# A kernel of resampled pointwise MLP and selective scan: D's row blocks in four places, S in two, `wtot` at slot 60, and a new slot plan

## What is computed

```python
def _L0(x):                                   # layer 0
    xu = upsample_rfft(x)                     # band-limited, twice per axis
    h = xu @ W1.T + b1                        # 96 -> 384
    h = coef[:, 0] + coef[:, 1] * h + coef[:, 2] * (h * h)
    h = h @ W2.T + b2                         # 384 -> 96
    return lpf_rfft(h)[..., ::2, ::2]         # back to 64 x 64
def _mamba(u):                                # layer 1, 4096 tokens in order
    xs, z = split(u @ W_in.T)                 # 192 + 192
    xc = silu(causal_conv3(xs) + conv_b)
    dt, Bm, Cm = split(xc @ W_x.T)            # 6, 16, 16
    delta = softplus(dt @ W_dt.T + b_dt)
    h = exp(delta * A) * h + delta * Bm * xc  # a scan over tokens, 192 x 16 states
    return ((h * Cm).sum(-1) + xc * D) * silu(z) @ W_out.T
x = x + _L0(_gn(x))                           # _gn: group norm, groups of 3 channels
x = x + _mamba(_gn(x))
```

## Time and profile before

| | |
|---|---|
| median of 3 runs | 6460.34 us (6443.52 to 6460.46) |
| the profiled execution | 6467.2 us; its span 6465.4 us |
| first `b` of the loop starts | 343.86 us |
| instructions | 99088 |
| mean granted TensorE clock | 0.951 |
| DVE scans | 3072, 1262 ns each |

### The profile page before, as it was taken

One profiled execution on the slowest core, in us unless ns is written; L12 is line 12 of the kernel. 1 busy time (PEld: TensorE's weight loads), 2 busy tenths in 40 slices (PEclk: granted clock), 3 DMA queues, 4 the chain that ended last, 5 costly groups with the idle time before them and its releaser, 6 DMA issues. The chain is left out here.

```text
span 6465.4 us, 99088 instructions
## 1 busy us (share of the span) xinstructions
PE 6103.6 (94%) x32316; PEld 3160.6 (49%) x32316; DVE 5686.3 (88%) x4459; ACT 5099.6 (79%) x8658; POOL 5211.7 (81%) x5092
## 2 busy tenths in 40 slices
PE   7999999999999999999999999999999999998776
PEld 5645545455454544545455544545545454454222
DVE  0089998999999999999989999898999989899998
ACT  4587888878788887878888788887878888786664
POOL 0078888888888888888888888888888888888988
PEclk8999999999999999999999999999999999998675
DMA  3276666666666667676666766666676666766553
GB/s 91 81 169 164 159 163 150 161 162 166 163 151 161 152 168 162 162 171 146 167 152 160 171 151 168 149 162 157 164 166 154 163 151 165 157 144 148 128 129 74
DMA packets 805826, 983.26 MB, mean 152 GB/s; under 512 B 391258, under 2 KB 417542, under 8 KB 805318
## 3 DMA queue, kind: packets, MB, share of 16 engines
q1 hardware_dynamic: 805318, 976.92, 64.3%
HBM read 717.71 MB, written 259.00 MB: 151 GB/s over the span
## 5 line engine op out<-in xcount | busy, mean ns | idle before, releaser
L1145 POOL TENSOR_TENSOR hc<-hs,cs 128x512 f32<-128x512 f32 x3072 | 3838.8, 1273 | 799.2 <-DVE hs L1104 467.2
L1104 DVE TENSOR_TENSOR_SCAN hs<-av,state,b 128x512 f32<-128x512 f32 x2688 | 3254.7, 1262 | 83.0 <-DVE b L1098 1.8
L974 ACT ACTIVATE av<-rep_d,nega 128x512 f32<-128x512 f32 x3072 | 2113.1, 713 | 34.4 <-DVE hs L1104 29.9
L1098 DVE TENSOR_TENSOR b<-rep_u,pb 128x1536 f32<-128x1536 f32 x1024 | 1802.5, 1760 | 249.7 <-PE pb L813 169.8
L822 PE MATMUL py<-hc,rsel 128*32 128x512 f32 x6144 | 1142.5, 634 | 64.6 <-POOL hc L1145 63.0
L738 PE MATMUL cb<-xu,w1a 96*128 96x392 f32 x2400 | 996.1, 517 | 23.1 <-ACT g L924 9.2
L743 PEld LDWEIGHTS cb<-w2c,g 128*98 128x98 f32 x9600 | 893.3, 169 | 163.2 <-issue 94.6
L743 PE MATMUL cb<-w2c,g 128*98 128x96 f32 x9600 | 917.2, 253 | 14.5 <-ACT g L924 11.7
L777 PE MATMUL cb<-xn,wtap 96*96 96x512 f32 x1536 | 737.4, 617 | 0.0
L924 ACT ACTIVATE g<-cb,b1a 128x392 f32<-128x392 f32 x1200 | 674.1, 579 | 66.8 <-PE cb L738 59.9
L738 PEld LDWEIGHTS cb<-xu,w1a 96*128 96x128 f32 x2400 | 417.3, 192 | 422.4 <-issue 231.4
(11 more groups left out here) (104 smaller groups left out, 6721.8 us busy)
## 6 DMA issues: line engine op xcount, KB each, us to landing
rep_d<-delta_scratch SPq DMA_DIRECT2D x512, 384.0 KB, 6.9
rep_u<-deltax_scratch SPq DMA_DIRECT2D x512, 384.0 KB, 6.6
cs<-c_scratch SPq DMA_DIRECT2D x512, 256.0 KB, 5.9
delta_scratch<-dlt SPq DMA_DIRECT2D x128, 384.0 KB, 3.1
deltax_scratch<-dlt SPq DMA_DIRECT2D x128, 384.0 KB, 7.7
t_scratch<-t1s SPq DMA_DIRECT2D x128, 300.0 KB
t1r<-t_scratch SPq DMA_DIRECT2D x160, 240.0 KB, 6.2
rr<-v_scratch SPq DMA_DIRECT2D x256, 150.0 KB
```

The lines of the kernel that those rows point to most:

```text
L974: act.activation(av[:, n % NAV, :], rep_d[:, k % 2, j, :], ACT.Exp, scale=nega[:, q, j:j + 1])\
L1098: dve.tensor_tensor(b3[:, :, :], rep_u[:, k % 2, 3 * hf:3 * hf + 3, :], pb[:, None, :].broadcast_to([128, 3, T]), ALU.mult).then_inc(dve_b ...
L1104: dve.tensor_tensor_scan(hs[:, n % NHS, :], av[:, n % NAV, :], b3[:, n % 3, :], start, ALU.mult, ALU.add)\
L1145: pool.tensor_tensor(hc[:, n % NHC, :], hs[:, n % NHS, :], cs[:, k % 2, g % NQ, :], ALU.mult)\
```

## The change

It sets other slots: X at 8 and 10, Z1 at 11, Z0 at 12, DBC at 14, S to slot 87, W from 105, D from 100 to 139, ACT's `xn` and `d` at 10 and 11, POOL's `bc` and `y` at 18, 22 and 17, 8; no slots are kept free. DVE's lag is 3. A new unringed step DW at slot 60 has POOL make `wtot`; DG waits for `act_w` alone, and the first D_lo waits for `pool_w`. D's row blocks take four places, two of `rr` and two of `xb`, loaded four ahead. `xs` alternates with a half of `x1s`, and `t1s` with `rr`, each with a semaphore of its own. At the start SP loads `ident`, x block 0, `up_w` and x block 1 first, PE begins the S steps of sample 0 when these are there, and PE's, ACT's and part of DVE's setup stands behind those steps.

```diff
@@ -35,13 +35,13 @@
...
-    "act": dict(xn=8, y=(18, 6), d=13, mid=23, batch=16),
+    "act": dict(xn=10, y=(18, 6), d=11, mid=23, batch=16),
...
-    "pool": dict(u=23, bc=(17, 20), y=(18, 9)),
-    "sp": dict(rd=(1, 2, 3, 4), ru=(7, 9, 11, 13), cs=(15, 16, 17, 18), dl=20, du=3, x1=19, out=23),
+    "pool": dict(u=23, bc=(18, 22), y=(17, 8)),
+    "sp": dict(rd=(1, 2, 3, 4), ru=(7, 9, 11, 13), cs=(15, 16, 17, 18), dl=21, du=4, x1=21, out=23),
...
-LAG = {"pe": 0, "act": 4, "dve": 2, "pool": 1, "sp": 1}
-UNRINGED = ("SLD", "WLD", "DLD", "WARM")
+LAG = {"pe": 0, "act": 4, "dve": 3, "pool": 1, "sp": 1, "bn": 3}
+UNRINGED = ("SLD", "WLD", "DLD", "DW", "WARM")
@@ -71,15 +71,16 @@
...
-S_LAST, W_FIRST, W_LAST, D_FIRST, D_LAST = 86, 106, 91, 101, 136
-X_AT, Z_AT, DBC_AT, DT_AT = (10, 7), (11, 11), 15, 18
-KEEP_FREE = tuple(range(9, 11))
+S_LAST, W_FIRST, W_LAST, D_FIRST, D_LAST = 87, 105, 87, 100, 139
+X_AT, Z_AT, DBC_AT, DT_AT = (8, 10), (12, 11), 14, 18
+KEEP_FREE = tuple(range(9, 9))
...
+DW_AT = 60
@@ -143,7 +144,7 @@
...
-        rows += [(D_FIRST - 6, ("DLD", 0)), (D_FIRST - 2, ("DG", 0))] + even(d_steps(), D_FIRST, D_LAST)
+        rows += [(DW_AT, ("DW", 0)), (D_FIRST - 6, ("DLD", 0)), (D_FIRST - 2, ("DG", 0))] + even(d_steps(), D_FIRST, D_LAST)
@@ -302,6 +303,7 @@
...
+        ld_s = sem("ld_s")
@@ -310,16 +312,16 @@
...
-        t1_st = sem("t1_st")
+        t1_st = [sem("t1_st0"), sem("t1_st1")]
...
-        rr_ld = [sem("rr_ld0"), sem("rr_ld1")]
+        rr_ld = [sem(f"rr_ld{p}") for p in range(4)]
...
-        xt_st = sem("xt_st")
+        xt_st = [sem("xt_st0"), sem("xt_st1")]
@@ -356,13 +358,24 @@
...
+        def rows_of(m):
+            return rr[:, m % 4] if m % 4 < 2 else xb[0:GW, m % 4 - 2]
+        def t1s_of(b):
+            return t1s[:, :, :] if b % 2 == 0 else rr[:, :, :, :].rearrange("w p h c -> w (p h) c")
+        def xs_of(b):
+            return xs[:, :] if b % 2 == 0 else x1s[:, 0, :]
...
-            (up_w[:, :, :], A["up_w"]), (up_h[:, :], A["up_h"]), (dn_h[:, :], A["dn_h"]),
-            (dn_w[:, :], A["dn_w"]), (ident[:, :], A["ident"]), (gavg[:, :], A["gavg"]),
+            (up_h[:, :], A["up_h"]), (dn_h[:, :], A["dn_h"]), (dn_w[:, :], A["dn_w"]), (gavg[:, :], A["gavg"]),
@@ -387,7 +400,7 @@
...
-                  alone([("WLD", 0), ("WG", 0)] + w_steps(), [("SLD", 0)] + s_steps()),
+                  alone([("WLD", 0), ("WG", 0)] + w_steps() + [("DW", 0)], [("SLD", 0)] + s_steps()),
@@ -396,8 +409,10 @@
...
-        starts = [SETUP_STEPS]
-        for plan in BEFORE:
+        N_FIRST = ringed(BEFORE[0])
+        starts = [0, N_FIRST + SETUP_STEPS]
+        for plan in BEFORE[1:]:
@@ -433,7 +448,7 @@
...
-        def run(when, unit_fn, step_fn, a_fn, c_fn):
+        def run(when, unit_fn, step_fn, a_fn, c_fn, setup_fn):
@@ -454,6 +469,8 @@
...
+                if s == -2:
+                    setup_fn()
@@ -475,6 +492,14 @@
...
+            def load_xb(x, b):
+                sp.dma_start(xb[:, b % 2], tok(xtok, x, b * T, T)).then_inc(xb_ld[b % 2], 16)
+            sp.dma_start(ident[:, :], A["ident"]).then_inc(ld_s, 16)
+            load_xb(0, 0)
+            sp.dma_start(up_w[:, :, :], A["up_w"]).then_inc(ld_s, 16)
+            load_xb(0, 1)
@@ -482,9 +507,6 @@
...
-            def load_xb(x, b):
-                sp.dma_start(xb[:, b % 2], tok(xtok, x, b * T, T)).then_inc(xb_ld[b % 2], 16)
@@ -493,7 +515,7 @@
...
-                sp.dma_start(rr[:, m % 2], src).then_inc(rr_ld[m % 2], 16)
+                sp.dma_start(rows_of(m), src).then_inc(rr_ld[m % 4], 16)
@@ -505,13 +527,14 @@
...
-                if name == "SLD":
+                if name == "SLD" and x > 0:
...
-                    sp.wait_ge(t1_st, count(t1_st, (x + 1) * 128))
-                    sp.sem_inc(sp_passed, 1)
+                    for p in range(2):
+                        sp.wait_ge(t1_st[p], count(t1_st[p], (x + 1) * 64))
+                        sp.sem_inc(sp_passed, 1)
@@ -519,11 +542,13 @@
...
-                    sp.wait_ge(xt_st, count(xt_st, (x + 1) * 128))
-                    sp.sem_inc(sp_passed, 1)
-                    for m in range(2):
+                    for p in range(2):
+                        sp.wait_ge(xt_st[p], count(xt_st[p], (x + 1) * 64))
+                        sp.sem_inc(sp_passed, 1)
+                    for m in range(4):
...
-                        load_xt(x, m)
+                        if m < 2:
+                            load_xt(x, m)
@@ -531,8 +556,8 @@
...
-                    sp.dma_start(dst, t1s[:, :, :].rearrange("p h c -> p (h c)"))\
-                        .then_inc(t1_st, 16)
+                    sp.dma_start(dst, t1s_of(b).rearrange("p h c -> p (h c)"))\
+                        .then_inc(t1_st[b % 2], 16)
@@ -553,13 +578,13 @@
...
-                    sp.dma_start(dst, xs[:, :]).then_inc(xt_st, 16)
+                    sp.dma_start(dst, xs_of(b)).then_inc(xt_st[b % 2], 16)
...
-                    if m + 2 < 2 * NC8:
+                    if m + 4 < 2 * NC8:
...
-                        load_rr(x, m + 2)
+                        load_rr(x, m + 4)
@@ -649,11 +674,12 @@
...
-            run(lambda row: row[0] + LAG["sp"], lambda s, k, n: None, step, a_part, c_part)
+            run(lambda row: row[0] + LAG["sp"], lambda s, k, n: None, step, a_part, c_part, lambda: None)
...
-            sp.wait_ge(xt_st, count(xt_st, NS * 128))
-            sp.sem_inc(sp_passed, 1)
+            for p in range(2):
+                sp.wait_ge(xt_st[p], count(xt_st[p], NS * 64))
+                sp.sem_inc(sp_passed, 1)
@@ -661,17 +687,22 @@
...
-            pe.wait_ge(ld_w, count(ld_w, 16 * len(loads)))
-            pe.wait_ge(setup_v, count(setup_v, 5))
-            for f in range(NF):
-                mm = pe.matmul(cb[0:C, 0, 0:C], g2[:, 0, f, 0:C], g2[:, 1, f, 0:C], start=(f == 0), stop=(f == NF - 1))
-            mm.then_inc(pe_conv, 1)
-            for f in range(NF):
-                mm = pe.matmul(cb[0:C, 1, 0:1], w2t[:, f, :], fcst[:, f:f + 1], start=(f == 0), stop=(f == NF - 1))
-            mm.then_inc(pe_conv, 1)
-            pe.transpose(cb[0:C, 2, 0:C], ident[0:C, 0:C], ident[0:C, 0:C]).then_inc(pe_conv, 1)
-            pe.wait_ge(setup_v, count(setup_v, N_SETUP))
-            pe.wait_ge(setup_a, count(setup_a, 2))
+            pe.wait_ge(ld_s, count(ld_s, 32))
+            def setup():
+                pe.wait_ge(ld_w, count(ld_w, 16 * len(loads)))
+                pe.wait_ge(setup_v, count(setup_v, 5))
+                for p in range(RING):
+                    pe.wait_ge(cb_free[p], count(cb_free[p], N_FIRST // RING))
+                for f in range(NF):
+                    mm = pe.matmul(cb[0:C, 0, 0:C], g2[:, 0, f, 0:C], g2[:, 1, f, 0:C], start=(f == 0), stop=(f == NF - 1))
+                mm.then_inc(pe_conv, 1)
+                for f in range(NF):
+                    mm = pe.matmul(cb[0:C, 1, 0:1], w2t[:, f, :], fcst[:, f:f + 1], start=(f == 0), stop=(f == NF - 1))
+                mm.then_inc(pe_conv, 1)
+                pe.transpose(cb[0:C, 2, 0:C], ident[0:C, 0:C], ident[0:C, 0:C]).then_inc(pe_conv, 1)
+                pe.wait_ge(setup_v, count(setup_v, N_SETUP))
+                pe.wait_ge(setup_a, count(setup_a, 2))
@@ -748,21 +779,23 @@
...
-                    pe.wait_ge(pool_w, count(pool_w, x * 2 + 2))
+                    pe.wait_ge(act_w, count(act_w, x * 2 + 2))
...
+                    if m == 0:
+                        pe.wait_ge(pool_w, count(pool_w, x * 2 + 2))
...
-                    pe.wait_ge(rr_ld[m % 2], count(rr_ld[m % 2], x * 128 + (m // 2 + 1) * 16))
+                    pe.wait_ge(rr_ld[m % 4], count(rr_ld[m % 4], x * 64 + (m // 4 + 1) * 16))
...
-                        mm = pe.matmul(o[:, j, :], rr[:, m % 2, j, :], dn_w[:, :], start=False, stop=(j == 3),
+                        mm = pe.matmul(o[:, j, :], rows_of(m)[:, j, :], dn_w[:, :], start=False, stop=(j == 3),
@@ -841,16 +874,15 @@
...
-            run(lambda row: row[0], unit, step, lambda st, k, n: None, c_part)
+            run(lambda row: row[0], unit, step, lambda st, k, n: None, c_part, setup)
...
-            act.wait_ge(ld_w, count(ld_w, 16 * len(loads)))
-            act.activation(nega[:, :, :], nega[:, :, :], ACT.Exp).then_inc(setup_a, 1)
-            act.activation(selb[:, :, :].rearrange("p q m -> p (q m)"), sels, ACT.Copy).then_inc(setup_a, 1)
-            act.wait_ge(setup_v, count(setup_v, N_SETUP))
-            n_dd = [0]
+            def setup():
+                act.wait_ge(ld_w, count(ld_w, 16 * len(loads)))
+                act.activation(nega[:, :, :], nega[:, :, :], ACT.Exp).then_inc(setup_a, 1)
+                act.activation(selb[:, :, :].rearrange("p q m -> p (q m)"), sels, ACT.Copy).then_inc(setup_a, 1)
+                act.wait_ge(setup_v, count(setup_v, N_SETUP))
@@ -897,8 +929,8 @@
...
-                        act.wait_ge(t1_st, count(t1_st, x * 128 + b * 16))
-                    out = t1s[:, :, :].rearrange("p (i r) c -> p i r c", r=2)[:, :, par, :]
```

(36 more changed lines are left out.)

## The result

The kernel before took 6456.8 us (median of the runs beside it), the changed kernel **6343.5 us** (6340.8 to 6346.5). The ratio is **0.9821, 95% interval 0.9801 to 0.9842**: 113 us less, where 155 were forecast. The profiled execution has a span of 6343.7 against 6465.4, 121.7 less; that is more than 113, because the profiled execution of before took 6467.2 us, 10.4 above its median, and that of the changed kernel 6345.5, 2.0 above.

The account below looks back on a forecast made before the run. DVE was taken as bound, needing 368.2 us of each 383.7 us sample, the rest mostly waits for PE. Savings of 140 (14 samples of 10), 5 (sample 14) and 10 (start) make 155: 6305 us, range 6240 to 6385.

Parts of the forecast that it names:

- the 15.5 us: DVE standing still in each full sample: 10.2 us for `pb`, 3.8 for row statistics, 1.5 for PAD.
- wtot at slot 60: DG no longer waits for POOL's `wtot`: 2.64 us of PE idle and 3.4 of lost clock removed, 6.0 a sample.
- Four places: D's row loads issued four steps ahead: `rr` wait of 2.3 us and its clock loss go, about 4.8 of PE.
- D over 40 slots, nothing kept free: PE's work in chunks 4 to 7 falls from about 189 to 182 us, where DVE needs 184.
- Statistics and PAD: Per sample, DVE's row-statistics waits fall from 3.8 us to 0.7, its PAD wait from 1.5 to 0.8.
- The stretch at slots 130 to 141: New worst stretch of PE late in the sample: slots 130 to 132 hold 8.1 us against 5.6; 1.5 stall.
- The start: S0 before the setup and loads: terms 7 + 3.6 − 2.5 + 3, sum 11, taken as 10 us saved.
- the smaller moves: POOL's `bc` and `y`, SP's `dl`, `du`, `x1` and `rep_u` shift slots: cost 0, bounds −0.5 and +1 us.
- A: Rival: the waits move into slots 120 to 141, a sample saves 6 us, kernel at 6364; chance 0.16.
- B: Rival: nearly all stall goes, 2 us a sample left, 210 saved, kernel at 6250; chance 0.13.
- D: Rival: DG or D steps wait for something else, only statistics and start gain, 50 us at most, 6430; chance 0.06.
- C: Rival: PE's clock drops in slots 75 to 99, losing 20 us of PE a sample, kernel at 6571; chance 0.05.

## Why the prediction was right or wrong

**What bounds the kernel, and the 15.5 us**: right. The floor of 368.2 us a sample was met at 368.1 with PE relieved; the three causes (`pb`, `bst`, PAD) are what stood there. Only the total is time, though; see statistics and PAD.

**wtot at slot 60**: right. Of the 6.0 us of PE that the step named, 2.7 reached the sample, and DG has no wait for POOL in the changed kernel.

**Four places**: right. 4.5 us a sample and no `rr` wait; the step named 4.8 us of PE.

These two parts give 7.2, the whole gain of a full sample; what the forecast added for the rest of the change came to nothing that the runs can tell.

**D over 40 slots, nothing kept free**: here a step failed, by what it left out. The prediction summed PE's work for chunks 4 to 7 alone, and expected nothing of the others. Chunks 4 to 7 did get 9.6 us shorter (198.1 to 188.5), nearly what the forecast gave the whole sample. But the same edit has `W_LAST` going from 91 to 87, and the prediction gave it no price: W's tail is packed into fewer slots ahead of 87, and chunks 0 to 3 got 2.4 longer (185.6 to 188.0). With 91 they are 2.2 shorter again. From the distances between `pb` and `pb` on PE, its idle time taken out, PE needs 139.0 us for the first 24 groups of a sample of the changed kernel (chunks 0 to 2), and 141.6 for the 24 from the second group on, where DVE takes 138.1 when PE is relieved (45.9 + 45.9 + 46.3); PE comes in ahead of DVE and goes out behind it, so the chunks themselves are 140.6. In chunks 4 to 7 the same distances give 185.2, where the prediction's step costs gave 182 against DVE's 184: 1.7% too low, and enough to put PE on the wrong side of DVE. The trace of before could have said so: the prediction's costs gave it 189 with the two waits, the distances 191.4 without any idle time.

**Statistics and PAD**: `bst` waits went as said (57.6 to 5.9 us in 13 samples), PAD from 22.7 to 19.5 and not to half. The failing step is that they were struck off the 15.5 one by one, as though each were time by itself. The old plan with its `bst` waits removed had them back as `pb` waits (86.7 to 121.6 us), the kernel without the PAD wait likewise (92.3 to 113.3). The step was worth at most the 0.7 a sample between those two kernels of the old plan, not 3.1, and 0.7 is within what two traces of one plan differ by.

**The stretch at slots 130 to 141.** The interval of slots 130 to 132 was forecast at 8.1 us; PE's timeline of sample 5, from one `pb` to the next:

```profile
2472.86 0.38 PE L846 MATMUL pb<-bc,selb 96*128 96x512 bf16 x1
...
2480.76 0.38 PE L846 MATMUL pb<-bc,selb 96*128 96x512 bf16 x1
```

7.90 us, and `b` behind it waits 1.31. The stall forecast for that stretch was 1.5; it is 2.1. That after it was forecast at 2 and is 1.7. The 3.3 in chunks 2 and 3 had no term but the 0.5 of unnamed stall. With it in that term's place the residue of 5.5 becomes 8.3. Some 1.2 of the 3.3 is W's tail packed ahead of slot 87 (2.1 stay with it at 91); the rest looks like the exchange for `bst`, since the old plan with the statistics at lag 3 has 1.9 at slots 54 to 69.

**The start**: forecast 10, measured 15.7. PE's timeline in the first stage answers to the earlier trace rows:

```profile
4.50 1.09 PE L737 MATMUL cb<-ident,xb 128*96 128x128 f32 x4 [4.50 <-DMA up_w<-in_up_w]
...
19.68 1.06 PE L737 MATMUL cb<-ident,xb 128*96 128x128 f32 x4 [9.43 <-DMA xb<-in_x]
...
39.55 1.06 PE L737 MATMUL cb<-ident,xb 128*96 128x128 f32 x4 [1.05 <-DMA xb<-in_x]
...
49.59 0.94 PE L763 MATMUL cb<-up_h,t1r 128*96 128x196 f32 x2
```

PE begins at 4.50 (5.5 forecast), its third block at 19.68 (20), and the blocks then follow at 4.0 us each (five from 19.68 to 39.55; 4.1 forecast). The setup behind S0 took 45.1 to 47.4. Three things were off. The D stage before the loop gained more (the kernel with the row places alone starts 6.6 us earlier, with DW as well 5.4; 3 forecast), and the first stage with two places for S gave 11.2 where the prediction's terms sum to 8.1 (7 + 3.6 − 2.5). And PE has a longer wait there, 7.51 us where before had 2.56 for `xt`, with the clock at 0.50 from 205.29 to 222.36 (the window's first row):

```profile
216.63 1.59 PE L763 MATMUL cb<-up_h,t1r 128*96 128x196 f32 x4 [7.51 <-DMA t1r<-t_scratch]
218.01 1.06 PE L794 MATMUL cb<-xt,wtot 96*96 96x256 f32 x2
```
```profile
205.29:222.36 17.07, 7.91 (x30) 6.92 (x31) 0.32 (x2) 2.88 (x8) 0.74 (x2) 0.50 0.43 105
324.75:348.64 23.89, 18.77 (x59) 10.21 (x58) 16.90 (x14) 14.64 (x24) 12.78 (x12) 0.50 0.86 203
```

With the old plan the first D step came at 211.49 instead of 218.01, yet the first `b` only 0.9 us sooner (327.29, 328.15), so that wait costs little by itself: 5.4 + 11.2 − 0.9 = 15.7.

**Sample 0** was counted as one more full sample, 10 us; it gave 1.4. The loss is in its first chunk: 56.9 us, and 49.7 with the old plan, while the other seven together gained. DVE's timeline in it:

```profile
328.15 1.76 DVE L1134 TENSOR_TENSOR b<-rep_u,pb 128x1536 f32<-128x1536 f32 x1 [3.18 <-DMA rep_u<-deltax_scratch]
...
342.43 1.76 DVE L1134 TENSOR_TENSOR b<-rep_u,pb 128x1536 f32<-128x1536 f32 x1 [3.22 <-PE pb L846]
...
351.87 1.76 DVE L1134 TENSOR_TENSOR b<-rep_u,pb 128x1536 f32<-128x1536 f32 x1 [3.37 <-PE pb L846]
```

and PE's:

```profile
339.60 1.06 PE L737 MATMUL cb<-ident,xb 128*96 128x128 f32 x4 [2.56 <-DMA xb<-in_x]
...
344.94 1.93 PE L855 MATMUL py<-hc,rsel 128*32 128x512 f32 x6
```

The first `b` waits for the load of `rep_u`, which still counts to the start, and PE for that of `xb`. From 324.75 to 348.64 the clock is at 0.50 (last row of the windows above), and two `pb` come over 3 us late: 6.6 of the 7.2 us. In the kernel with the old plan the first `b` waits 0.23, for `pb`, and no other over 0.6 in that chunk. So the prediction's "cost 0, bounds −0.5 and +1" for the smaller moves, `rep_u` named among them, does not hold here for the new plan as a whole; that SP's slots are the cause is not shown. In samples 1 to 13 DVE shows no wait for `rep_u`. Sample 14 gained 9.1 where 5 were forecast, and the row places alone give 10.8 (362.6).

**The sum**: 15.7 + 1.4 + 94.0 + 9.1 + 1.4 = 121.6 of span, against 10 + 10 + 130 + 5. The result, 6343.5, is inside 6240 to 6385 but outside the forecast's own 6275 to 6335; of what is missing, 36 us are in the full samples (130 − 94) and 9 in sample 0; the start and sample 14 gave 10 more than forecast. Those 10 are luck as far as the number goes: they hide part of what the full samples lack.

**The rivals.** A (waits move into slots 120 to 141, 6364) was half right: the waits moved, but into chunks 2 and 3 more than there, and the saving of 7.2 a sample lies between A's 6 and the forecast's 10. B (6250) is what the kernel does and more when PE is relieved of a third of W_2. D fell: no PE row names SP's loads for the D steps, and all that DG's copy costs is the wait for `cst`, 0.8 us a sample, which did not lengthen the sample. **C** (the clock) fell with its mechanism. It said that 40 us at half clock would cost 20 of PE in each sample; without any WARM there were 17.6 us a sample (229.0 / 13), and with 11.4 us less of WARM on PE the samples kept their length; 40 us were not reached in any run. The Trainium skill ("TensorE: Matmul & The Clock Gate", What's actually happening) says that the throttled state is the default and that activity releases the throttle. The trace agrees: clock 0.50 after idle slots in the kernel without WARM. What neither the sentence nor the argument for C asks is whether PE's time is needed in that stretch; here it wasn't.

What stays **open**: which slot of the new plan brings the late loads before and in sample 0 (no run took them apart); how much of the start's gain is the order of the loads and how much the two places for S (together 11.2 us to the first `b`, from 338.45 to 327.29, when they are added to the kernel with DW and the row places; not tried apart); and what half clock would cost with PE's work unchanged.

## What to carry to other kernels

Where two engines both need nearly the whole period (PE is busy 369.4 us a sample here, 4801.83 / 13, and DVE's floor is 368.2), a wait that is taken from one is paid back at its next handover from the other; only what gives the late engine room shortens the period, by less work or by work moved from its full slots to its empty ones. So sum the other engine's work over every stretch that an edit touches, also the one that an edit packs tighter to make room elsewhere, and take it from distances between repeated instructions rather than from durations of single ones. And a lower clock is priced by who waits for the engine in that stretch, not by its length.
